# A decoder kernel: a causal mask moved into the relative scores' product, and each engine's order of steps written as a table

## The reference, cut to what matters

```python
q, k, v = heads(x @ W_q), heads(x @ W_k), heads(x @ W_v)      # 16 heads of 8
scores = einsum('bhqd,bhkd->bhqk', q, k)
rel_idx = pos[None, :] - pos[:, None] + (n - 1)
scores += einsum('bhld,lrd->bhlr', q, rel_emb[rel_idx])
scores = where(pos[None, :] > pos[:, None], -inf, scores)
attn = softmax(scores / sqrt(HD)); out = (attn @ v) @ W_o + b_o
```

## Time and profile before

| | us |
|---|---|
| runs | 781.44 in the median (780.78, 781.44, 786.85) |
| the profiled execution, first to last instruction | 780.6 |
| PE busy | 663.0 |
| DVE busy | 549.0 |
| ACT busy | 444.9 |
| POOL busy | 442.9 |

### The profile page before, as it was taken

One profiled execution on the slowest core, in us unless ns is written; L12 is line 12 of the kernel. 1 busy time (PEld: TensorE's weight loads), 2 busy tenths in 40 slices (PEclk: granted clock), 3 DMA queues, 4 the chain that ended last, 5 costly groups with the idle time before them and its releaser, 6 DMA issues.

```text
span 780.6 us, 22984 instructions
## 1 busy us (share of the span) xinstructions
PE 663.0 (85%) x8876; PEld 497.6 (64%) x8876; DVE 549.0 (70%) x1471; ACT 444.9 (57%) x1092; POOL 442.9 (57%) x614
## 2 busy tenths in 40 slices
PE   5988896889999996999978989878988889949990
PEld 2665663567777784776456667738955567736990
DVE  4867867976888766787398999543557799952654
ACT  2225644578788763667465767355727667622671
POOL 2258836985777733333155988344666668553550
PEclk8558966999999996899998999688999999957995
DMA  9139000000000000000008600004115481013112
GB/s 298 33 138 229 9 3 0 2 2 2 2 2 3 2 2 1 3 3 3 2 3 139 189 3 4 2 28 99 45 53 180 158 263 43 3 52 91 56 37 88
DMA packets 50793, 44.30 MB, mean 57 GB/s; under 512 B 15904, under 2 KB 41376, under 8 KB 50176
## 3 DMA queue, kind: packets, MB, share of 16 engines
q1 hardware_dynamic: 48448, 38.24, 17.9%
q0 software_dynamic: 2240, 4.60, 1.7%
HBM read 29.95 MB, written 12.88 MB: 55 GB/s over the span
## 4 chain that ended last, share of the span: by engine, by line
PE 55%; DVE 16%; issue 9%; POOL 7%; ACT 6%; DMA 4%; SPq 1%; DVEq 0%; ACTq 0%; POOLq 0%
PE bank L1002 5%; PE bank L981 5%; PE bank L989 4%; PE bank L1070 3%; PE bank L1187 3%; PE bank L1262 3%; PE bank L1269 3%; PE bank L1095 2%; PE bank L1136 2%; DVE sm L1751 2%; PE bank L1120 2%; PE bank L895 2%; DVE X L1687 2%; DVE mx L1753 2%; ACT pT L1357 2%
## 5 line engine op out<-in xcount | busy, mean ns | idle before, releaser
L2173 POOL TENSOR_TENSOR sm<-sm,mx 128x512 f32<-128x512 f32 x80 | 84.5, 1059 | 36.5 <-DVE mx L1753 36.2
L1353 ACT ACTIVATE pr<-sm 128x512 f32<-128x512 f32 x112 | 70.9, 634 | 31.6 <-POOL sm L2173 26.1
L1357 ACT COPY pT<-bank 128x512 f32<-128x512 f32 x112 | 65.5, 585 | 33.7 <-PE bank L989 32.5
L989 PE MATMUL bank<-W,pr 128*128 128x128 f32 x448 | 74.8, 292 | 8.3 <-ACT pT L1357 6.0
L2140 POOL TENSOR_SCALAR veps<-mv 128x1 f32<-128x1 f32 x104 | 23.5, 226 | 90.9 <-DVE mv L1683 90.6
L2168 POOL TENSOR_TENSOR pairs<-KS,quad 128x512 f32<-128x512 f32 x48 | 51.7, 1077 | 35.5 <-ACT KS L1336 35.3
L981 PE MATMUL bank<-pairs,Q 64*64 64x256 f32 x896 | 67.1, 418 | 3.8 <-DVE sm L1745 2.7
L989 PEld LDWEIGHTS bank<-W,pr 128*128 128x128 f32 x448 | 52.5, 147 | 18.4 <-issue 10.5
L2141 POOL TENSOR_TENSOR rstd<-veps,W 128x1 f32<-128x1 f32 x104 | 58.9, 567 | 8.7
L1002 PEld LDWEIGHTS bank<-VX,pT 64*64 64x64 f32 x3072 | 53.4, 142 | 10.2 <-issue 4.5
L1002 PE MATMUL bank<-VX,pT 64*64 64x9 f32 (+1 forms) x3072 | 56.7, 204 | 1.8 <-ACT pT L1357 1.1
(11 more groups left out here) (399 smaller groups left out, 1850.4 us busy)
## 6 DMA issues: line engine op xcount, KB each, us to landing
big<-gup SPq DMA_DIRECT2D x4, 1024.0 KB, 10.1
rel_scratch<-G SPq DMA_DIRECT2D x16, 256.0 KB, 2.6
W<-small SPq DMA_DIRECT2D x1, 3206.5 KB, 12.7
big<-early SPq DMA_DIRECT2D x2, 1557.0 KB, 8.3
slots_x<-zero SPq DMA_DIRECT2D x2, 1472.0 KB, 21.0
big<-down SPq DMA_DIRECT2D x8, 256.0 KB, 8.9
QM<-rel_scratch SPq DMA_DIRECT2D x16, 128.0 KB, 2.7
PM<-rel_scratch SPq DMA_DIRECT2D x16, 128.0 KB, 2.8
```

What stands on the lines that cost most here:

```text
L989: last = pe.transpose(tile(ps, p), pr[:, u % 2, 4 * h + p, :, :].rearrange("p b k -> p (b k)"), ident)
L1353: act.activation(pr[:, u % 2, 4 * h:4 * h + 4, :, :].rearrange("p g b k -> p (g b k)"), sm[:, 2 * (u % 2) + h, :], ACT.Exp, scale=a["scale ...
L1357: act.copy(pT[:, u % 2, 4 * h:4 * h + 4, :], bank[BK[f"tu{h}"]][:, :].rearrange("p (h n) -> p h n", h=4)).then_inc(pt_ready, 1)
L2173: tt(v, v, bc(mx[:, slot, :], [P, 8, S], 2), ALU.subtract).then_inc(pcentered, 1)
```

## The change

**The mask.** rel_scratch's rows are 528 numbers apart (RELW) instead of 512; one DMA fills the 16 numbers behind each row with -1e30 once, early on, from the new table `beyond`. The first factor of the relative product is no longer Q but RQ, a copy of the tile's split q to which POOL adds `spot` (new step `rq`, placed between `act.q` and `pe.rel`): the feature rows of the other heads, which are zero in a split q, get a one-hot row of the token's place in its sequence. The second factor is relc instead of relp: the same numbers, and in the rows of the other heads -1e30 for each distance that this token can't have. So the product itself writes -1e30 where another head's number stood, the skewed load brings it to the keys k > q, and the minimum with `causal` goes away in a3 (the local layers keep theirs). `rel_tables` builds the tables on DVE in top1_ffn, ahead of its first copy; `rel_with_mask` makes relc (two operations of 128x512) where `rel_rows` stood before.

**Landing buffers.** Four tiles instead of two: RBs gets two more, in the part of `big` behind the top-2 experts' weights, and a load waits for the additions of four tiles before. RQ and relc lie there too.

**The tables.** The planners with their durations, ranks and heads are gone. ORDER holds, for each engine, the steps of parts 0 and 1 and of the local layers (written with a dot) in one sequence; ORDER3 does for part 2. `follow` reads them. The steps are the same ones, 684 on PE, 545 on ACT, 464 on DVE and 304 on POOL in ORDER, and 170, 137, 107 and 96 in ORDER3, of which the eight `rq` on POOL are new; their sequence is another. Against the planner's, a step of ORDER stands 1.3 places away on PE, 1.1 on ACT and DVE and 2.6 on POOL in the mean, and one of ORDER3 2.0, 1.8, 1.1 and 5.9.

**Small ones.** `exps` starts true, so that L1381 doesn't load the table before the first step of the local layers. The statistics of gelu's second half wait for their tile's norm.

```diff
-RELOAD, LOCAL_PATIENCE = 1.5, 0.1
...
-def local_plan():
...
+ORDER = {
+    "pe": (
...
+        ".ua .hn .fx .va .ug .st .dn .ua .out .hn .fx .fy .ug .st .ua .dn v .fy k .hn .dn k .ug .ua .fx .fy "
+        ".fx .dn .fy v .fy q v sc .fx v k .fx .fx q tu k sc q v q tu v k va tu sc k fo tu v y k tu sc tu k va "
...
+    "act": (
...
+        "ex q pt pt o ex x pt ex q o pt ex ex x pt o pt x ex o ex pt o pt x .k x .q o x x .q .k .rn .q x .tk "
...
+    "dve": (
...
+        ".ff .mx .x1 .ua .sum .sum .st .fr .hn .x1 .fr .st .ff .hn .x1 .ua .st .ff .hn .ua .x1 .fr .st .ua "
+        ".hn v .ff .fr .ua .ff .fr .fr v .fr v .ff .ff sc sc .ff v v sc v sc on sc sc re v fi sc on sc on re "
...
+ORDER3 = {
+    "pe": (
+        "y y y x y k v x q y x v sc k y rel x q y v x y k v q rel k x q rel k x v sc v tu q rel tu k sc rel q "
+        "tu x va sc tu rel k fo tu va y q tu sc fo k tu va tu q x rel q fo y sc rel tu y va tu x sc tu x va q "
...
+    "pool": (
+        "xb xb xb xb rs xb xb rs rs kv xb rq xb xb xb rs xb rs xb rq rs kv rq rs kv rs kv ce xb rq ce ce rq "
...
+def follow(engine, text, chains):
+
+    local, planned, turns = [], [[] for _ in chains], []
+    queues, taken = [chain_steps(stages) for stages in chains], {}
+    for word in text.split():
+        n = taken[word] = taken.get(word, -1) + 1
+        if word[0] == ".":
+            n += MT * LOCAL_ONLY.get(word[1:], 0)
+            local.append((word[1:], n // MT, n % MT, n))
+            turns.append("local")
+            continue
+        for part, queue in enumerate(queues):
+            own = queue.get(f"{engine}.{word}", [])
+            if n < len(own):
+                planned[part].append(own[n])
+                turns.append(part)
+                break
+            n -= len(own)
+    return local, planned, turns
...
+RELW = 512 + 16
...
+        RBs += [room(NE3 * WIDE3 + (3 + 2 * i) * 512, 2 * 512, "p (m n) -> p m n", m=2) for i in range(2)]
...
+            sp.dma_start(scratch.ap().rearrange("m (p n) -> p m n", n=RELW)[:, :, 512:RELW], bc(beyond[:, :], [P, MB, RELW - 512], 1)).then_inc(beyond_in, 16)
...
-                    if b >= 4:
-                        sp.wait_ge(rel_added, 2 * (t - 1))
+                    if t >= 4:
+                        sp.wait_ge(rel_added, 2 * (t - 3))
...
                     if step == "rel":
-                        pe.wait_ge(q_split, at_["q", t])
+                        pe.wait_ge(rq_ready, 8 + t + 1)
+                        pe.wait_ge(relc_ready, 2)
                         for c in range(2):
-                            mm(fill(6 + c, rel_ready)[:, :], own_q[:, c, :],
-                               relp[:, :, :].rearrange("p h k -> p (h k)"), start=True, stop=True).then_inc(rel_full, 1)
+                            mm(fill(6 + c, rel_ready)[:, :], RQ[:, t % 2, c, :, :].rearrange("p b s -> p (b s)"),
+                               relc[:, c, :, :].rearrange("p h k -> p (h k)"), start=True, stop=True).then_inc(rel_full, 1)
...
-                exps = False
+                exps = True
...
+            def rel_with_mask():
+                for c in range(2):
+                    last = stt(relc[:, c, :, :], relp[:, :, :], w("par16", c, c + 1), bc(early_keys[:, c, :], [P, 8, S], 1),
+                               ALU.mult, ALU.add)
+                last.then_inc(relc_ready, 1)
...
-                                link(tt(dst, dst, bc(w("causal"), [P, 8, S], 1), ALU.min))
...
+                    if step == "rq":
+                        if t >= 2:
+                            pool.wait_ge(rel_full, 2 * (t - 1))
+                        pool.wait_ge(q_split, q_count(name, t))
+                        pool.wait_ge(relc_ready, 2)
+                        tt(RQ[:, t % 2, :, :, :], Q[:, q_slot(name, t), :, :].rearrange("p c (b s) -> p c b s", b=2),
+                           bc(spot[:, :, :], [P, 2, 2, S], 2), ALU.add).then_inc(rq_ready, 1)
```

382 lines of the change are left out of this document (122 added, 260 removed), and 43 rows, old and new, of tables (ORDER, ORDER3).

## The result

| | before | after |
|---|---|---|
| runs of the comparison, median us | 784.14 (780.78 to 787.70, 4 runs) | 762.75 (757.73 to 764.53, 4 runs) |
| the profiled execution, first to last instruction | 780.6 | 762.7 |

The ratio is 0.9727, with a 95% interval of 0.967 to 0.978: faster by 2.7%. The gain is larger than forecast: 21.4 us between the medians and 17.9 us between the profiled executions, where the two terms of the sum said 12.

The account below looks back on a forecast made before the run. PE, busy 663.0 of 780.6 us, was taken as the bound, with holes in a3. The 780.6 us span less 6 (a3) less 6 (ORDER) gave 768.6, so 769.4 in the runs' median; own range 763 to 773.6, wide range 757 to 779.

Parts of the forecast that it names:

- 6 us for a3: Fourth attention, 571 to 642 us: PE's 59.83 us of work at 92% density takes 65.0 us instead of 71.
- 6 us for ORDER: Parts 0, 1 and local layers, up to 504 us: the new step order shortens PE's holes; bounds 0 to 18.
- (c): Rival: thin holes halved and drains shortened, clock able to carry it; 18 us from ORDER, 6 from a3; 757.4; chance 0.16.
- tile 4's store does not wait, so SyncE's path gives 7 us: In a3, five relative products before the first value product keep SyncE going; last adds and maxima end at 634.3, not 641.6.
- 1 us of spare against PE's path: In a3, SyncE's path was said to have 1 us to spare against PE's, an argument against padded stores setting the pace.
- the term taken as nothing: Padded rows in a3: slower store issue could cost SyncE 0.33 us per tile, 2.7 over eight; nothing was taken.
- 1 for the table load: Junction of x0 and local layers: ACT no longer reloads its table (1.28 us from 122.87); 1 us counted.
- 2 for the rank tables at the start of part 1: Drain from 290 us: rank_tables come behind both halves of a1's first scores instead of delaying the second; 2 us counted.
- 3 for thin holes: Up to 504 us: 36.5 us of PE's idle time lie in thin holes; a twelfth, 3 us, counted as gain.
- (a): Rival: ORDER brings nothing and only a3 gains its 6 us; 775.4; chance 0.16.
- (b): Rival: first query sum behind POOL's norms, or padded stores, leave a3 2 of 6 us, 2 from the rest; 777.4; chance 0.09.
- (d): Rival: in the local layers PE meets one more 1.17 us wait per tile, 18.7 us over sixteen; 794; chance 0.09.

Follow-up runs that it names:

- before_no_min: Kernel before with only a3's causal minimum left out (mask missing from the output); a3's additions take 43.2 us, profiled span 776.3 us.
- two_buffers: Kernel after with two landing buffers for the relative scores instead of four; a3's additions take 43.1 us, profiled span 767.0 us.
- a3_planner: Kernel after with the planner's old order in the fourth attention's table, query sums on POOL kept; a3's additions take 52.5 us, profiled span 780.2 us.
- no_exps: Kernel after with ACT's table load at the start of the local layers put back; local layers take 134.5 us, profiled span 761.7 us.
- a3_min_back: Kernel after with a harmless DVE minimum behind each of a3's 16 additions; additions take 47.3 us, whole 756.78 us, run once.
- sp_ahead: Kernel after with SyncE issuing the next tile's stores before this tile's loads; ratio to before 0.989, a3's additions over 50.2 us.
- a3_only: Kernel after with the planner's old order in parts 0 and 1, fourth attention all new; 772.68 us, ratio to before 0.989.

## Why the prediction was right, step by step

**The sum.** It was right in direction and in both causes, and its size is partly luck. Of 6 us for a3 4.6 came, of 6 us for ORDER 11.5 to 13, so two errors of opposite sign stand in the 12 us, which were 17.9 in the trace. The measured 762.75 us is 6.7 us from the forecast and 5.4 from rival (c), 757.4; that it lies in the stated range is owed to the range's lower end, which was set to take in half of (c).

**The minimum.** Its steps hold but one: no minimum, and DVE busy for 28.6 us in the 41.5 of the additions (in the 50 us for which 28 was said it is 36.7, since x3's work moves in behind); the last addition starts 129.5 us after L1082's first product where it was 135.1 after L1166's. The tables added on DVE cost nothing, as said: DVE is busy for 3.5 us more in the stretch up to a3's first addition, its wait in front of the top-1 experts' first copy falls from 9.3 to 6.6 us, and the stretch keeps its length (87.9 and 88.0). The forecast was 6 us for a3, limited by PE's density. From 571 to 642 us that is 91%, as said, though not for the same work; within the additions PE is busy for 37.57 of 41.52 us, 90%. The stretch of a3 and x3 gave 3.9 us idle and 4.6 in length. Too large by a third: 6 us were taken from 571 to 642 us, but part of that is the fill of the stage, ahead of the first addition, where nothing was to be had (the first store comes 0.7 us later after the load of the experts' results, 14.1 instead of 13.4). The additions by themselves gave 5.7.

Two slips in the working changed nothing. The load of the eighth tile, 7.7 us after 623.5, is due at 631.2, not 631.5. And "the last a3 add near 633" takes only one of the two gains of 6 us off 639.3; it came at 620.5, 13.2 us earlier by what lies ahead of L1082 and 5.6 by what lies behind.

The runs put most of the gain in the additions on the minimum: put back, it costs all 5.7 us; taken out of the kernel before, it gives 4.1, and the 1.6 us between are inside the scatter of the eight kernels without it. For PE's idle time in a3 and x3 the minimum accounts for some 2 to 3 of the 3.9 us (14.8 us with it put back, 13.5 with it alone taken out); the rest is not assigned.

**ORDER3 and the buffers.** The step "tile 4's store does not wait, so SyncE's path gives 7 us" is right in what it shows (no pause, 5.70 us per tile against 5.5 forecast and the limit of 5.8), but not shown in what it is worth: before_no_min still has 8.5 us from tile 3's store to tile 4's and has most of the gain without it. The bound on the other side, SyncE's loop, was seen coming as "1 us of spare against PE's path"; DVE's 9.2 us of waits for loads point to that.

**rq and the padded rows.** 0.73 us each where 0.65 was taken (between 0.455 and 1.077), and 0.7 us late for tile 0, inside the 0.5 to 1.2. PE waited 0.5 us for it, once. For the padded rows, an issue of a store takes 435 ns (430 before), a load 588 (597), the landing 2.8 us (2.7): the term taken as nothing was nothing. The rule on rows that do not start at a 256 B boundary, in the Trainium skill, "DMA: Bandwidth & Descriptors", section "How a descriptor splits into AXI transactions", has no visible effect here: by it nine transactions stand for eight in three stored rows of four, and the medians of the trace differ by 0.1 us at most.

**ORDER.** This is the term that was mis-sized: 6 us forecast, 11.5 us of idle time in the trace (12.2 in the mean of all kernels), and 13 by the times of the GELU product (366.9 to 353.6) and L1082 (504.2 to 491.0; the stretch to 504 was to end near 498). Of its three parts, 1 for the table load, 2 for the rank tables at the start of part 1 and 3 for thin holes, the load is at most 0.9, and the start of part 1 did give 2.3 (whether by the rank tables was not tried). The junction of x0 and the local layers gives some 5, more than the 1 that I gave it, and the thin holes of the local layers and part 1 the rest. The rows to see it were there: the drain from 100 to 130 us was counted with its 7.2 us of idle, and then only the table load taken off it, because the waits in it (L895 for the norm, 2.9 us; L1095 for ACT, 2.7 us, one of them) were read as dependencies, though they were places in a queue: with the new order both waits are gone, and the same work is done.

**The rivals.** (a) and (b) are out. (c), with 18 us from ORDER and 6 from a3, came nearest in size, and half of its reason was right: thin holes and the drain at the junction did shrink, by 11.5 us instead of 18. The other half, "the clock could carry it", was not: in the sum over the whole kernel the clock gave 0.8 us. (d), one more wait per tile in the local layers, is the opposite of what happened: 8.3 us per tile against 9.1.

## What to carry to other kernels

Split each stretch, cut at events, into work, clock and idle before comparing two traces: here the idle part of one stretch mostly repeats within 1 or 2 us from execution to execution (the local layers' within 0.9, part 1's within 5), while the clock part of the whole moves by up to 24. Take the clock part as an upper bound, since the work part moves against it. When an order is written anew, look where two stages meet: waits at the head of a queue there are often a matter of places. And of an operation that is moved ahead on an in-order engine (a store on SyncE, a small sum on POOL), ask first what stands behind it: both experiments that put a wait in front of ready work lost some 9 us in a3's additions. When the profile names no releaser for a wait, compare the end of each producer with the start of the operation: the query sums' wait looked like one for a free buffer and was one for their own input.

## What the runs showed of the hardware

- PE's granted clock falls at other moments in executions of kernels whose instructions are the same up to there. Between the last local projection and the first GELU product it cost 11.2 us in after, two_buffers, a3_planner and (with the table load) no_exps, 6.4 in a3_min_back and 4.9 in sp_ahead, which differ only behind that.
- With idle products the clock was 0.99 from 100 to 130 us, where it had been 0.60, at 8.0 us of added work in the local layers for 6.4 us of clock. Part of that difference may be the execution's: a3_only, with the same order and no idle products, has 0.83 there, before_no_min 0.58.
- A row pitch of 2112 B instead of 2048 B changed neither the issue nor the landing of stores and loads between SBUF and DRAM by more than 0.1 us in the median.
- An addition on POOL of 128x256 numbers takes 0.73 us, beside 0.455 for 128x128 and 1.077 for 128x512.
